# The query squares behind the down products: one stage of a fused attention and expert kernel is reordered

## The reference

```python
x = x + tanh(g_xattn[0]) * attention0(layernorm(x), ctx)      # scores of ctx with itself, softmax, times x
x = x + tanh(g_ffn[0])   * linear(layernorm(x))               # weight made of 4 bit planes, and a bias
x = x + tanh(g_xattn[1]) * attention1(layernorm(x), ctx)      # 16 heads of 128, RMS norm on queries and keys
x = x + tanh(g_ffn[1])   * experts(layernorm(x), topk_idx)    # 16 experts, top 4, inner width 352
```

## Time and profile before

| | |
|---|---|
| median of 3 runs | 1579.97 us (1579.19 to 1580.41) |
| the profiled execution, its own time | 1579.88 us |
| its span, first to last instruction | 1578.0 us |
| TensorE busy, of the span | 1493.5 us (95%) |
| VectorE, ScalarE, GpSimd busy | 1041.7, 1000.5, 824.8 us |
| mean granted clock of TensorE | 0.988 of full |
| packed steps | t = 20 to 51, 544 to 1343 us |

### The profile page before, as it was taken

The page is one execution under the profiler, slowest core; times in us unless marked ns, Lnnn a source line. Parts: engine busy times, 40 slices in busy tenths (PEclk is TensorE's granted clock), DMA queues, the critical chain, the costliest instruction groups (busy, mean ns, idle before and its releaser), DMA issues.

```text
span 1578.0 us, 24699 instructions
## 1 busy us (share of the span) xinstructions
PE 1493.5 (95%) x8506; PEld 1272.8 (81%) x8506; DVE 1041.7 (66%) x2061; ACT 1000.5 (63%) x2238; POOL 824.8 (52%) x662
## 2 busy tenths in 40 slices
PE   5889889999999999999999999999999999999997
PEld 3777768888888788888888888888888888888886
DVE  7776556666666766666666666666666665677665
ACT  6864446767666666666666666666656665566654
POOL 3444235555554465655656556574646554664331
PEclk9999979999999999999999999999999999999999
DMA  6310001111111233343433334343333331321002
GB/s 234 121 47 14 1 21 54 41 48 41 54 41 54 97 116 124 107 136 104 140 114 122 119 112 143 103 133 114 129 104 127 129 108 54 94 87 34 8 1 80
DMA packets 53369, 138.60 MB, mean 88 GB/s; under 512 B 5312, under 2 KB 5312, under 8 KB 53248
## 3 DMA queue, kind: packets, MB, share of 16 engines
q1 hardware_dynamic: 49488, 124.71, 23.5%
q0 software_dynamic: 3760, 12.32, 2.8%
HBM read 122.60 MB, written 14.42 MB: 87 GB/s over the span
## 4 chain that ended last, share of the span: by engine, by line
PE 77%; DVE 9%; ACT 5%; POOL 4%; issue 3%; DMA 1%; POOLq 0%; ACTq 0%; SPq 0%; DVEq 0%
PE j_bank L431 10%; PE j_bank L433 10%; PE j_bank L432 10%; PE w_bank L431 9%; PE w_bank L433 8%; PE w_bank L432 8%; PE t_bank L510 5%; POOL sqs_lo L1379 3%; PE s_bank L431 3%; PE s_bank L433 3%; PE s_bank L432 3%; PE t_bank L586 2%; PE t_bank L587 2%; PE t_bank L576 2%; DVE qT_lo L976 2%
## 5 line engine op out<-in xcount | busy, mean ns | idle before, releaser
L812 ACT ACTIVATE prob<-s_bank,neg_bias,q_scale 128x512 f32<-128x512 f32 x256 | 198.5, 777 | 293.2 <-DVE neg_bias L1202 292.8
L976 DVE TENSOR_TENSOR probT_lo<-t_bank,probT_hi 128x512 fp32r<-128x512 f32 x264 | 179.0, 688 | 212.0 <-ACT probT_hi L714 209.5
L1241 DVE SCALAR_TENSOR_TENSOR x_sb<-w_bank,inv_sum,x_sb 128x512 f32<-128x512 f32 x256 | 187.2, 741 | 1.9 <-PE w_bank L433 1.9
L1186 DVE TENSOR_REDUCE neg_max<-s_bank 128x1 f32<-128x512 f32 x256 | 168.8, 679 | 5.9 <-PE s_bank L433 5.9
L510 PE MATMUL t_bank<-ident,prob 128*128 128x128 f32 x1024 | 154.5, 273 | 3.9 <-DVE probT_lo L976 2.0
L714 ACT CAST probT_hi<-t_bank 128x512 fp32r<-128x512 f32 x264 | 153.2, 594 | 1.6 <-PE t_bank L510 1.6
L1379 POOL TENSOR_TENSOR sqs_lo<-xn,sqs_hi 128x512 fp32r<-128x512 f32 x64 | 82.8, 1294 | 128.6 <-ACT xn L870 128.5
L431 PE MATMUL j_bank<-wkv_lo,cT_hi 128*128 128x256 f32 x512 | 146.0, 285 | 3.7 <-issue 2.4
L433 PE MATMUL j_bank<-wkv_hi,cT_lo 128*128 128x256 f32 x512 | 146.0, 285 | 0.0
L432 PE MATMUL j_bank<-wkv_hi,cT_hi 128*128 128x256 f32 x512 | 145.8, 285 | 0.0
L510 PEld LDWEIGHTS t_bank<-ident,prob 128*128 128x128 f32 x1024 | 122.4, 140 | 24.1 <-issue 3.3
(11 more groups left out here) (241 smaller groups left out, 4491.1 us busy)
## 6 DMA issues: line engine op xcount, KB each, us to landing
stage<-w SPq DMA_DIRECT2D x96, 256.0 KB, 2.7
xnT_raw<-w_gu SPq DMA_DIRECT2D x31, 704.0 KB, 4.0
cT_raw<-w_gu SPq DMA_DIRECT2D x31, 704.0 KB, 4.4
xnT_raw<-w_dn SPq DMA_DIRECT2D x16, 768.0 KB, 4.3
cT_raw<-w_dn SPq DMA_DIRECT2D x15, 768.0 KB, 4.7
planes<-bits SPq DMA_DIRECT2D x16, 512.0 KB, 3.9
y<-stage SPq DMA_DIRECT2D x31, 256.0 KB
x_sb<-x SPq DMA_DIRECT2D x5, 1024.0 KB, 10.2
```

Source lines behind the costliest of these rows:

```text
L812: nc.scalar.activation(prob[:, i, :], s_bank[i % 2][:], ACT.Exp, bias=neg_bias[:, u % 2, i:i + 1], scale=q_scale[:, u % 2, i:i + 1], accum ...
L976: return nc.vector.tensor_tensor(dst, src, hi, ALU.subtract)
L1186: nc.vector.tensor_reduce(neg_max[:, u % 2, i:i + 1], s_bank[i % 2][:], AX_X, ALU.max, negate=True).then_inc(own_max, 1)
L1241: nc.vector.scalar_tensor_tensor(out=here, in0=w_bank[0 if packed else i % 2][:], scalar=inv_sum[:, w % 2, i:i + 1], in1=here, op0=ALU.mul ...
```

## The change

In packed steps, TensorE's `query_squares` moves from in front of `turn_rows` to behind `project_down`. ScalarE's `rows_to_hi` moves ahead of `softmax(0)`. On VectorE, in packed steps, `gate_up_lo`, `inverses` and `copy_y` move ahead of `squares_out`, and `rows_to_lo` stands between `squares_out` and the two `shift`s. On GpSimd `take_rows(b + 1)` moves ahead of `query_scale`. Unpacked steps keep their order.

```diff
--- before.py
+++ after.py
@@ -666,9 +666,12 @@
 
                 scores(0)
                 scores(1)
-                query_squares()
+                if not packed:
+                    query_squares()
                 turn_rows()
                 project_down()
+                if packed:
+                    query_squares()
                 values()
                 key_value(0)
                 probs(0)
@@ -918,11 +921,11 @@
                 if t and fresh(t):
                     split_wkv(t)
                 gate_up_hi(0)
+                rows_to_hi()
                 softmax(0)
                 if not packed:
                     values_hi()
                 softmax(1)
-                rows_to_hi()
                 if fresh(w):
                     split_wo(w)
                 if t and fresh(t):
@@ -1308,17 +1311,25 @@
 
                 maximum(0)
                 maximum(1)
-                squares_out()
-                shift(0)
-                shift(1)
+                if packed:
+                    gate_up_lo()
+                    inverses()
+                    copy_y()
+                    squares_out()
+                    rows_to_lo()
+                    shift(0)
+                    shift(1)
+                else:
+                    squares_out()
+                    shift(0)
+                    shift(1)
+                    inverses()
                 if t == 0:
                     experts()
                 if t == 1:
                     places()
                 if t == 2:
                     tokens()
-                gate_up_lo()
-                inverses()
                 if t == T0 - 2:
                     dve.wait_ge(w_added, 4 * (LAST[0] + 1))
                     batch_moments(0, NMOMENTS)
@@ -1330,8 +1341,6 @@
                         nc.vector.tensor_scalar(here, here, mean_var[:, 0, i, 0:1], rstd[:, 0, i:i + 1],
                                                 ALU.subtract, ALU.mult).then_inc(rows_ready, 1)
                     nc.vector.memset(h_row[:, I:], 0.0).then_inc(pad_ready, 1)
-                copy_y()
-                rows_to_lo()
                 take(0)
                 take(1)
                 values_lo()
@@ -1512,6 +1521,8 @@
 
                 if t and fresh(t):
                     lower_wkv(t)
+                if up:
+                    take_rows(b + 1)
                 query_scale()
                 if t == T0 - 2:
                     inverse_deviations(NMOMENTS // NT, 0)
@@ -1519,8 +1530,6 @@
                     lower_wo(w)
                 if t and fresh(t):
                     lower_wq(t)
-                if up:
-                    take_rows(b + 1)
                 take_y(0)
                 take_y(1)
                 gate_up_lo()
```

## The result

| | changed kernel | kernel before |
|---|---|---|
| median us | 1589.93 of 5 runs (1585.85 to 1590.88) | 1579.97 of 5 runs (1577.95 to 1580.41) |
| ratio, 95% interval | 1.0062 [1.0047, 1.0077] | |
| span of the profiled execution | 1589.0 us | 1578.0 us |
| mean granted clock of TensorE | 0.985 | 0.988 |
| a packed step, the middle one of steps 21 to 50 | 25.33 us | 25.01 us |

What follows compares the result with a forecast made beforehand. TensorE was taken to bound the kernel, busy 1493.5 of 1578.0 us. Terms 7.4 + 0.8 - 1.7 = +6.5 us on the profiled execution's 1579.88 gave 1586.4, and 0.1 for the median made 1586.5; range 1583.3 to 1591.0.

Steps and rivals of the forecast that it cites:

- Its first step: Packed steps on TensorE: the transposes now wait for VectorE's `add(3)`, which ends 0.26 us behind GpSimd's `sqs_lo`.
- The addition behind `sqs_lo`: Transposes behind `scores(1)`: their wait for the last addition into x ends 0.26 us later than the old wait, per step.
- The hand-over: TensorE's start after the addition: 0.09 us taken, between 0.05 and 0.15, so 0.04 more per step.
- The neighbours: TensorE from squares or transposes to `values()`: 3.47 us in the new order against 3.53, giving back 0.06 per step.
- The step: Each packed step longer by 0.26 + 0.04 - 0.06 = 0.24 us (0.20 to 0.30); times 31, +7.4 us.
- Step 20: No `project_down` there; squares that filled the transposes' wait are paid in full: +0.8 us, up to 1.1 if `probs(0)` waits.
- The late weights: Two steps with late `gate_up_hi(1)` weights: transfer issued 0.6 earlier, consumer reached 0.24 later, -1.7 us (0 to -2.1).
- The scale chain: Squares to `softmax(0)`: done at 875.6, `probs(0)` reached at 876.7; margin 1.1 us, no cost; 0.1 left at step 20.
- ScalarE, GpSimd, SP: nothing: Moved `rows_to_hi`, `take_rows`, `y_store` and the weights' transfer were to cost TensorE nothing.
- the first (the gap goes, 1551 us): Rival: transposes don't wait for `add(3)`, 28 us gained, 1551 us, if that addition ends by 867.8; chance 0.04.
- The second, no difference: Rival: addition comes 0.2 sooner, or hand-over and late transfers give back the rest: 1578 to 1583 us; chance 0.07.
- The third rival: `take_rows` beside VectorE's gate-weight lowering delays the scale chain; `probs(0)` stops TensorE, 0.35 per step, 1597 us; chance 0.06.

Runs made afterwards that it cites:

- experiment 1: Changed kernel with VectorE's `add(3)` ahead of `inner_lo` in packed steps: 1567.34 us, ratio 0.9917.
- Experiment 4: Kernel before with only TensorE's `query_squares` moved behind `project_down`, other engines as before: 1588.07 us, ratio 1.0046.
- Experiment 5: Changed kernel with the wait for `w_added` asked first in `turn_rows`, ahead of `rows_in` and `h_lo`: 1587.38 us, ratio 1.0054.
- Experiment 9: Kernel before with TensorE's squares moved, except in step 20, and ScalarE's `inner_hi` ahead of `query_squares`: 1543.54 us, ratio 0.9782.
- experiment 8: Kernel before with TensorE's squares moved and ScalarE's `inner_hi` ahead of `query_squares`, other orders as before: 1546.45 us, ratio 0.9789.
- experiment 6: Changed kernel with step 20 alone having its squares in front of the transposes again: 1588.31 us, ratio 1.0059.
- experiment 7: Changed kernel with ScalarE's `inner_hi` ahead of `query_squares` and step 20's squares in front of the transposes again: 1548.37 us, ratio 0.9803.
- experiment 11: Kernel before with the changed orders of VectorE, ScalarE and GpSimd alone, TensorE's order as before: 1579.81 us, ratio 1.0008.
- experiment 3: Kernel before with ScalarE's `inner_hi` ahead of `query_squares`, TensorE's squares where they were: 1576.43 us, ratio 0.9979.
- experiment 10: Changed kernel whose step 20 makes the squares twice, first unused in the gap ahead of `turn_rows`: 1588.90 us, ratio 1.0067.
- experiment 2: Changed kernel with ScalarE's `inner_hi` ahead of `query_squares`: 1548.87 us, ratio 0.9804.

## Why the prediction was right

The forecast was 1586.5 us and slower; measured 1589.93, inside the range of 1583.3 to 1591.0 and below the 1590.3 of its sum's upper end. Its first step, that the transposes wait for the addition and that this ends 0.26 us behind `sqs_lo`, is shown by experiments 1 and 4: take the addition away and 0.7 of the 1.17 goes; make TensorE's move alone and the loss is there. Its terms, one by one:

- **The addition behind `sqs_lo`, 0.26 per step.** Measured 0.25 to 0.27 in all steps from 21 on.
- **The hand-over, 0.04 (ends 0 and 0.10).** Measured 0.10, the far end. I took 0.09 us from the addition to the transposes, nearer to what `sqs_lo` had at the same place; what counted was the row of the same pair of instructions, 0.15 in step 20. Experiment 5 shows that 0.09 of it hangs on where the wait stands among three. This is the term that was mis-sized in the step: 0.06 by 31, 1.9 us.
- **The neighbours, -0.06.** From the transposes to `values()` it is 3.38 us, against 3.53 from the first square to `values()` before, and 0.08 more for the first product of `values()`: -0.07.
- **The step, 0.24.** These rows give 0.29 for step 33, and all steps in the mean 0.32, just above the upper bound of 0.30. The last 0.03 wasn't traced.
- **Step 20, 0.8 (up to 1.1).** Measured 2.5. The squares behind the wait cost 0.88, about as worked out; the other 1.6 are the fall of the clock, which the prediction had nowhere. Experiment 9 gives back both together (25.67 us in experiment 8, 23.19 in 9), experiment 6 all but the 0.9 of the late scale chain. The wait at `probs(0)` for which I had left a margin of 0.1 doesn't come in the changed kernel, where TensorE itself is late by the squares and the lower clock; in experiments 6, 7 and 11, where it isn't, it is 0.5 us.
- **The late weights, -1.7 (to -2.1).** Measured -2.5. The long steps had cost 2.8, more than the two waits of 2.1 in the earlier trace rows showed, and so more came back than the term's end of 2.1. The issue is earlier, as forecast (first row before, second after):

```profile
872.63 0.35 SPq L364 DMA_DIRECT2D xnT_raw<-w_gu  x1
...
878.09 0.35 SPq L364 DMA_DIRECT2D xnT_raw<-w_gu  x1
```

  That is 4.99 us behind the start of the scores' last product before and 4.47 after, 0.52 earlier where 0.6 was forecast. In the three traces with the squares in front and steps of 25.0 us (before, experiments 3 and 11) long steps cost 2.8, 1.1 and 1.4 us, in the five with the squares behind and 25.3 us (after, experiments 4, 5, 6 and 10) 0.3 at most. So it goes with the place of the squares; that it is through the earlier issue is argued.
- **The scale chain, margin 1.1.** `softmax(0)` is done at 881.48 + 0.19 = 881.67, `probs(0)` starts at 882.85: 1.18. `softmax(0)` starts 2.6 us later behind the scores than before, where 2.4 was forecast, and the squares 2.98 behind `sqs_lo`, where 2.9 was.
- **ScalarE, GpSimd, SP: nothing.** Experiment 4 is 1.9 us below the changed kernel and its interval overlaps the other's; experiment 11 finds no difference.

The two errors, +1.9 and +1.7, point the same way, and the landing term gives 0.8 back. That makes 2.8 of the 3.4 us by which the median lay above the forecast, and what is left of the steps (9.9 us instead of 7.4, less the 1.9) the other 0.6. The mechanism was right. That the time stayed within the sum's bounds in spite of the missing 1.6 us is luck in part: the late weights gave back more than they were put at.

Of the rivals, the first (the gap goes, 1551 us) was refuted for this change and its condition was right: "where that addition ends by 867.8, 1.1 us sooner than it does". In experiment 2 it ends before the last product of the scores, and the time is 1548.87. The rule of the Trainium skill (Perfetto Trace Analysis, Optimization Strategy) to make the awaited dependency earlier holds for the second wait as well as for the first; what the named releaser alone doesn't give is how far. The second, no difference, is out: the ratio's interval [1.0047, 1.0077] leaves it no room. The third rival had GpSimd's gather hold back VectorE's lowering of the gate weights. In the rows after they overlap from 876.75 to 877.16, and the lowering takes 1.62 us against 1.61. So the estimate of 0.2 us did not show for a gather. The prediction had read the rule on the shared ports (the Trainium skill, SBUF — State Buffer, Who interferes with whom) too widely: a VectorE instruction with two SBUF inputs contends there only with a GpSimd instruction that reads SBUF, and the section infers that the making of a transfer's descriptors needs the write side. The trace agrees with that, by the 1.62 against 1.61 us.

## What to carry to other kernels

Where an engine's queue is in order, moving the work that waits only uncovers the next wait: before moving it, list what every instruction that comes to stand first waits for and when each of these is done, and move the latest of them too. Here the change cost 10 us, the producer's move alone gave 3, none of it in the gap, and the two together 31. Then look at the granted clock wherever the move leaves only transposes and small products between two wide ones (128x512): behind the one such stretch here it was half for 3.4 us. And leave out each follower's edit that nothing on the bounding engine asks for.

## What was not expected of the hardware

- The order in which an instruction's three waits are asked for: TensorE starts 0.15 us after the releasing VectorE instruction with its wait last, 0.10 with it second, 0.06 with it first.
- TensorE's clock fell with the engine busy 3.83 of 4 us and then without a gap up to the fall, and each fall lasted 3.4 us. It didn't fall at a gap of 1.17 us followed by transposes and down products, 30 times in a row.
- The profile put a wait of 0.47 us down to "issue" (30 times, experiment 1) though by the code and the times it was VectorE's lowering that released it, 0.10 earlier.
